# One exponential over four score tiles instead of two, and new slots for the order of the other work

## The reference

```python
q = (x @ Wq.T + bq).reshape(B, S, H, Dh)          # H = 16 heads, Dh = 8
v = (x @ Wv.T + bv).reshape(B, S, H, Dh)
buckets = sum over 6 hyperplanes of (qa . plane >= 0) * 2**n
scores = einsum('bhsd,bhtd->bhst', q, q) / sqrt(128)
attn = softmax(scores * (62 + same_bucket), axis=-1)
out = einsum('bhst,bhtd->bhsd', attn, v)
# per batch: x = x + layernorm(attention(layernorm(x)))
h = silu(tlin(x, w1, s1)) * tlin(x, w2, s2)       # 512 wide
h = gelu(tlin(h, h1, s)); h = gelu(tlin(h, h2, s))
# x = x + layernorm(tlin(h, w3, s3)), the input of the FFN being layernorm(x)
```

## Time and profile before

| | |
|---|---|
| three runs | 1417.3, 1417.64 (median), 1419.8 us |
| the profiled execution, its time | 1414.98 us |
| its span, first to last instruction | 1412.9 us |
| time outside the span | 2.1 us |
| mean granted TensorE clock | 0.972 |
| start of T0 of batch 0; last T63 | 28.16; 1321.3 us |
| a batch in the middle (batch 10, T0 to T0) | 81.24 us |

### The profile page before, as it was taken

How to read it: one execution, slowest core, us unless ns; L and a number is a source line. 1 busy time by engine, 2 the same in 40 slices (tenths; PEclk the granted TensorE clock), 3 DMA queues, 4 the chain that set the end, 5 groups by cost and what they waited for, 6 DMA issues and landing times. The chain is left out here.

```text
span 1412.9 us, 19983 instructions
## 1 busy us (share of the span) xinstructions
PE 1239.0 (88%) x5430; PEld 525.6 (37%) x5522; DVE 1228.3 (87%) x4013; ACT 1086.0 (77%) x1477; POOL 1241.7 (88%) x275
## 2 busy tenths in 40 slices
PE   4656899998989899998999999898999889898997
PEld 1211334343433434334343433434343333433343
DVE  5988999999999999999999999999999899989420
ACT  2353778879797987979788797979789797878852
POOL 2789999999999999999999999999998999999810
PEclk9877899999999999999999999999999999999999
DMA  4645444453545354354534544354444435442100
GB/s 112 186 119 150 106 123 125 118 149 94 150 118 149 95 138 135 111 135 123 143 99 126 149 112 134 113 154 111 124 127 117 141 102 143 118 131 86 53 8 8
DMA packets 89472, 167.20 MB, mean 118 GB/s; under 512 B 18192, under 2 KB 54288, under 8 KB 89360
## 3 DMA queue, kind: packets, MB, share of 16 engines
q1 hardware_dynamic: 89252, 165.62, 42.1%
q10 hardware_dynamic: 108, 0.30, 0.1%
HBM read 150.39 MB, written 15.47 MB: 117 GB/s over the span
## 5 line engine op out<-in xcount | busy, mean ns | idle before, releaser
L943 POOL TENSOR_TENSOR logits<-max_row,logits 128x4096 f32<-128x4096 f32 x128 | 1139.2, 8914 | 44.1 <-DMA max_row<-max_scratch 42.1
L776 DVE CUSTOM_DVE_ANT_0 logits<-s_bank,coeff 128x512 f32<-128x512 f32 x1024 | 691.6, 676 | 0.0
L999 ACT ACTIVATE logits<-logits 128x1024 f32<-128x1024 f32 x512 | 508.8, 1048 | 50.4 <-POOL logits L943 49.2
L726 DVE TENSOR_SCALAR coeff<-brow,bcol 128x516 bf16<-128x516 bf16 x1024 | 480.0, 469 | 68.2 <-PE s_bank L532 46.7
L532 PE MATMUL s_bank<-mov_stack,stat_stack 128*128 128x512 bf16 x932 | 329.9, 395 | 54.9 <-DVE rowmax L776 45.8
L552 PE MATMUL aux_bank<-logits,v_pad 128*32 128x512 f32 x2048 | 252.5, 611 | 37.9 <-ACT logits L999 30.2
L664 PE MATMUL f_bank<-hid_a,h_sb 128*128 128x512 f32 x512 | 246.4, 593 | 0.9 <-DVE hid_a L865 0.8
L674 PE MATMUL f_bank<-hid_b,h_sb 128*128 128x512 f32 x512 | 241.7, 598 | 3.6 <-ACT hid_b L1114 3.6
L532 PEld LDWEIGHTS s_bank<-mov_stack,stat_stack 128*128 128x128 bf16 x1024 | 99.5, 99 | 354.3 <-DVE rowmax L776 218.3
L1019 ACT COPY oT<-aux_bank 128x512 f32<-128x512 f32 x64 | 37.2, 582 | 157.4 <-PE aux_bank L552 150.3
L674 PEld LDWEIGHTS f_bank<-hid_b,h_sb 128*128 128x128 f32 x512 | 96.8, 192 | 89.3 <-issue 78.2
(11 more groups left out here) (105 smaller groups left out, 961.7 us busy)
## 6 DMA issues: line engine op xcount, KB each, us to landing
max_row<-max_scratch SPq DMA_DIRECT2D x128, 512.0 KB, 4.1
brow<-bucket_scratch SPq DMA_DIRECT2D x63, 522.0 KB, 6.4
mov_stack<-q_scratch SPq DMA_DIRECT2D x192, 96.0 KB
stat_stack<-q_scratch SPq DMA_DIRECT2D x189, 96.0 KB
max_scratch<-rowmax_T SPq DMA_DIRECT2D x512, 1.0 KB
q_scratch<-q_parts SPq DMA_DIRECT2D x16, 384.0 KB, 6.4
x_in<-in_x SPq DMA_DIRECT2D x16, 256.0 KB, 4.3
q_scratch<-q_parts SPq DMA_DIRECT2D x16, 256.0 KB, 7.0
```

What stands on the lines that cost most here:

```text
L726: nc.vector.tensor_scalar(coeff[:, k % 3, :].rearrange("p (r n) -> p r n", r=ROW_RUNS), brow[:, h // 4 % 2, h % 4, :, 0:RUN], bcol[:, b % ...
L776: nc.vector.tensor_tensor_reduce(out=logits[:, ring(b, k), :], in0=tile_bank(k)[:], in1=coeff[:, k % 3, 0:SEQ], scale=float(E) ** -0.5, sc ...
L943: nc.gpsimd.tensor_tensor(tiles, max_row[:, m % 2].unsqueeze(2).broadcast_to([P, GROUP, ST, SEQ]), tiles, ALU.subtract).then_inc(below_max ...
L999: nc.scalar.activation(logits[:, first:first + 2, :], logits[:, first:first + 2, :], ACT.Exp, scale=-1.0).then_inc(probs_done, 1)
```

## The change

One exponential covers the four tiles of a head: two instructions of 2048 columns to a group where there were four of 1024. PE's wait for them counts accordingly. Most slots have new values. The slots of work that the prediction speaks of:

```diff
-COPY_LAG = 35
+COPY_LAG = 36
-X_LOAD_SLOT = 14
+X_LOAD_SLOT = 29
-X_MOMENTS_SLOT = 42
+X_MOMENTS_SLOT = 38
-X_NORM_SLOT = 49
+X_NORM_SLOT = 48
-Q_SLOT = 60
+Q_SLOT = 59
-ATT_NORM_SLOT = 28
+ATT_NORM_SLOT = 27
-Y1_PREPARE_SLOT = 35
+Y1_PREPARE_SLOT = 36
 Y1_NORM_SLOT = 36
-END_STATS_SLOT = 44
+END_STATS_SLOT = 43
-END_PREPARE_SLOT = 50
+END_PREPARE_SLOT = 48
-END_NORM_SLOT = 58
+END_NORM_SLOT = 52
-EXP_SLOTS = (12, 13, 14, 15)
+EXP_SLOTS = (13, 15)
-GATE_SLOTS = (43, 44, 49, 50)
-UP_SLOTS = (47, 48, 51, 52)
+GATE_SLOTS = (44, 45, 49, 50)
+UP_SLOTS = (46, 47, 51, 52)
-FIRST_HIDDEN_SLOTS = (57, 57, 58, 60, 62, 62, 64, 64, 65, 67, 70, 73, 74, 74, 75, 75)
+FIRST_HIDDEN_SLOTS = (57, 57, 58, 60, 61, 61, 63, 64, 64, 67, 70, 72, 73, 73, 75, 75)
-SILU_SLOTS = (41, 47)
-MULTIPLY_SLOTS = (47, 47, 52, 52)
-OUTPUT_SLOTS = (102, 104, 105, 105)
+SILU_SLOTS = (44, 47)
+MULTIPLY_SLOTS = (46, 47, 52, 52)
+OUTPUT_SLOTS = (101, 102, 105, 105)
-STORE_SLOT = 4
-LOAD_SLOT = 5
-Q_STORE_SLOT = 24
+EXP_TILES = ST
+STORE_SLOT = 1
+LOAD_SLOT = 4
+Q_STORE_SLOT = 31
...
-                first = ring(b, m * GT) + 2 * n
-                nc.scalar.activation(logits[:, first:first + 2, :], logits[:, first:first + 2, :],
+                first = ring(b, m * GT) + EXP_TILES * n
+                nc.scalar.activation(logits[:, first:first + EXP_TILES, :], logits[:, first:first + EXP_TILES, :],
...
-                    for n in range(GT // 2):
+                    for n in range(GT // EXP_TILES):
```

More of the change, by code:

```diff
@@ L52 @@
 EPS = 1e-5
-GATE_SLOTS = (43, 44, 49, 50)
-UP_SLOTS = (47, 48, 51, 52)
-FIRST_HIDDEN_SLOTS = (57, 57, 58, 60, 62, 62, 64, 64, 65, 67, 70, 73, 74, 74, 75, 75)
-SECOND_HIDDEN_SLOTS = (81, 81, 82, 82, 82, 82, 86, 88, 88, 88, 91, 91, 92, 95, 95, 98)
-SILU_SLOTS = (41, 47)
-MULTIPLY_SLOTS = (47, 47, 52, 52)
-OUTPUT_SLOTS = (102, 104, 105, 105)
+GATE_SLOTS = (44, 45, 49, 50)
+UP_SLOTS = (46, 47, 51, 52)
+FIRST_HIDDEN_SLOTS = (57, 57, 58, 60, 61, 61, 63, 64, 64, 67, 70, 72, 73, 73, 75, 75)
+SECOND_HIDDEN_SLOTS = (81, 81, 82, 82, 82, 82, 86, 88, 90, 90, 90, 91, 93, 94, 96, 97)
+SILU_SLOTS = (44, 47)
+MULTIPLY_SLOTS = (46, 47, 52, 52)
+OUTPUT_SLOTS = (101, 102, 105, 105)
 FIRST_GELU_SLOTS = (65, 70)
@@ L73 @@
 PV_LAGS = (36, 36, 37, 37)
-COPY_LAG = 35
+COPY_LAG = 36
 TRANSPOSE_LAG = 39
 DIVIDE_LAGS = (38, 39)
-X_STATS_SLOT = 33
-X_MOMENTS_SLOT = 42
-X_PREPARE_SLOT = 41
-X_RSTD_SLOT = 47
-X_NORM_SLOT = 49
+X_STATS_SLOT = 32
+X_MOMENTS_SLOT = 38
+X_PREPARE_SLOT = 39
+X_RSTD_SLOT = 40
+X_NORM_SLOT = 48
 XNT_COPY_SLOT = 53
 XNT_SLOT = 58
-Q_COPY_SLOT = 57
-Q_SLOT = 60
-Q_HIGH_SLOT = 56
+Q_COPY_SLOT = 56
+Q_SLOT = 59
+Q_HIGH_SLOT = 55
 V_SLOT = 32
@@ L93 @@
 Q_REST_SLOT = 61
-PROJ_SLOT = 26
-BITS_SLOT = 26
+PROJ_SLOT = 27
+BITS_SLOT = 27
 Q_MIDDLE_SLOT = 59
@@ L98 @@
 BCOL_COPY_SLOT = 28
-Q_LOW_SLOT = 62
+Q_LOW_SLOT = 63
 ROW_SLOT = 42
@@ L103 @@
 ATT_STATS_SLOT = 24
-ATT_MOMENTS_SLOT = 25
-ATT_PREPARE_SLOT = 27
-ATT_RSTD_SLOT = 24
-ATT_NORM_SLOT = 28
-RESIDUAL_SLOT = 31
-Y1_STATS_SLOT = 32
-Y1_MOMENTS_SLOT = 33
-Y1_PREPARE_SLOT = 35
-Y1_RSTD_SLOT = 39
+ATT_MOMENTS_SLOT = 26
+ATT_PREPARE_SLOT = 26
+ATT_RSTD_SLOT = 28
+ATT_NORM_SLOT = 27
+RESIDUAL_SLOT = 30
+Y1_STATS_SLOT = 33
+Y1_MOMENTS_SLOT = 35
+Y1_PREPARE_SLOT = 36
+Y1_RSTD_SLOT = 37
 Y1_NORM_SLOT = 36
@@ L117 @@
 FFN_SLOT = 38
-END_STATS_SLOT = 44
+END_STATS_SLOT = 43
 END_MOMENTS_SLOT = 51
-END_PREPARE_SLOT = 50
+END_PREPARE_SLOT = 48
 END_RSTD_SLOT = 53
-END_NORM_SLOT = 58
-Y2_SLOT = 56
+END_NORM_SLOT = 52
+Y2_SLOT = 59
 SUB_SLOT = 8
-EXP_SLOTS = (12, 13, 14, 15)
+EXP_SLOTS = (13, 15)
 S_BANKS = 4
@@ L131 @@
 GT = GROUP * ST
-STORE_SLOT = 4
-LOAD_SLOT = 5
-Q_STORE_SLOT = 24
-FIRST_XNT_SLOT = 17
-FIRST_Q_STORE_SLOT = 36
-X_LOAD_SLOT = 14
-ROW_STORE_SLOT = 46
+EXP_TILES = ST
+STORE_SLOT = 1
+LOAD_SLOT = 4
+Q_STORE_SLOT = 31
+FIRST_XNT_SLOT = 16
+FIRST_Q_STORE_SLOT = 33
+X_LOAD_SLOT = 29
+ROW_STORE_SLOT = 45
 STACK_SLOT = 8
-FFN_LOAD_SLOT = 7
+FFN_LOAD_SLOT = 9
 FFN_LOAD_STEP = 3
 X_RES_SLOT = 49
-OUT_SLOT = 61
+OUT_SLOT = 63
 def sandwich_kernel(nc, x, wqT, bq, wvT, bv, hyper_blocks, hyper_bias, w1T, w2T, h1T, h2T, scales, w3T, w3_s, out):
@@ L548, in weigh_values @@
                         pe.wait_ge(att_done, b * QUADS + quad)
-                    pe.wait_ge(probs_done, b * (TILES // 2) + (quad + 1) * QT // 2)
+                    pe.wait_ge(probs_done, (b * TILES + (quad + 1) * QT) // EXP_TILES)
                 for hh in range(4):
```

## The result

The changed kernel takes 1449.91 us (median of 5 runs, 1448.26 to 1455.58) against 1417.3 us (5 runs, 1417.02 to 1419.8): a ratio of 1.0226 [1.0207, 1.0245], 32.6 us more. The forecast was 1428 with a range of 1407 to 1440. The sign of the forecast was right; the loss is three times the 11 us that it had. The profiled execution is the longest of the five, 1455.58 us, so shares and places are read from it, and sizes per batch from its usual batches.

The account below looks back on a forecast made before the run. No engine fills a batch; waits tie POOL (m0 to m2), ACT (to SQRT) and DVE (T54 to T8) into a loop. Twelve batches of 0.9 us plus small terms gave +11 us: 1428 us, range 1407 to 1440.

Parts of the forecast that it names:

- ACT from the second normalisation to SQRT: +0.6 us: On ACT, two long exponentials behind the normalisation replace three short ones, so SQRT comes 0.59 us late per batch.
- The exponentials: On ACT, a merged exponential of 2048 columns takes 1.91 us; a batch costs ACT 1.5 us less.
- T54 to T62: On DVE after SQRT, a late `xnT` copy and q matmul make it wait for S60 to S62: +0.5 us a batch.
- The load of x: On SP, moved behind m2's broadcast, so m0's broadcast lands sooner: -0.2 us a batch.
- T38: PE's transposes come late and DVE waits 0.7 us, hidden in what it waits at T44 and T54 now.
- The `end_rstd` wait: A sign in the changed profile: this wait above 1.2 us in most batches; its absence would speak against the forecast.
- A broadcast late by under 1 us is covered: At m5, behind the `x_res` load: costs nothing, as the scaling no longer holds POOL up before m6.
- (2): Both late terms, T54 to T62 and the stretch to SQRT, fall away: no change, 1417 us; chance 0.11.
- (3): Only the T54 to T62 term falls away: +6 us, 1423 us; chance 0.15.
- (4): The wait at T38 is longer than DVE's spare time and adds 0.7 us: 1438 us; chance 0.07.
- (1): Waits at T44 and T54 were the real loss, cleared by ACT's 1.5 us: 1397 us, or 1407 with half; chance 0.27.
- (5): A long exponential costs two short pitches, stretch to SQRT +1.0 us: 1433 us; chance 0.40 shared with the forecast.

Follow-up runs that it names:

- kernel 1: Changed kernel plus one tiny exponential of one column ahead of the second normalisation's wait for the bias, to load the table there: 1427.88 us, ratio 1.0062.
- kernel 5: Kernel before with only the exponentials merged over four tiles, at slots 12 and 14, other slots as before: 1429.83 us, ratio 1.0075.
- kernel 7: Changed kernel with the tiny exponential, the `x_res` load early, and the scaling of `ffn` back behind m4's exponentials (slot 58): 1420.4 us, ratio 1.0015.
- kernel 10: Kernel before with only SQRT moved ahead of the normalisation of x on ACT (slot 50 to 48): 1419.16 us, ratio 1.0002.
- kernel 2: Changed kernel with only the load of `x_res` back ahead of m5's maxima stores (slot 46 instead of 49): 1447.92 us, ratio 1.0209.
- kernels 2 and 3: Changed kernel with the `x_res` load early: alone 1447.92 us; in 3 together with the tiny exponential ahead of the bias wait, 1425.5 us.
- kernels 9 and 11: Against the kernel before: 9 merges only each group's last two exponentials and moves the load of x, 1414.41 us; 11 also puts SQRT first, 1412.66 us.
- kernel 8: Changed kernel with every long exponential cut back into two short ones side by side, all slots as changed: 1456.67 us, ratio 1.0272.
- 4, normalisation one slot sooner: Kernel before with only the second normalisation moved from slot 36 to 35, ahead of m2's first exponential: 1459.14 us, ratio 1.029.

## Why the prediction was wrong

The loop in four pieces, us, medians of batches 2 to 12 from the timelines. A tile starts here with DVE's multiplication of its bank (L776), and "bias" is the end of POOL's `att_bias` for the second normalisation.

| kernel | m0's subtraction to bias | bias to T54 | T54 to next T8 | T8 to m0's subtraction |
|---|---|---|---|---|
| before | 32.29 | 20.30 | 21.17 | 7.27 |
| changed | 32.31 | 22.30 | 21.67 | 7.24 |
| 1, load warmed up | 32.33 | 20.88 | 21.67 | 6.92 |
| 5, long ones alone | 32.88 | 20.38 | 21.09 | 7.91 |
| 7, scaling back | 32.29 | 20.88 | 21.06 | 7.10 |
| 10, SQRT first | 32.31 | 20.08 | 21.40 | 7.26 |

**The step that failed** is "ACT from the second normalisation to SQRT: +0.6 us", in the sentence "The rest is the same work in the same order". The work in front of the stretch was not looked at. I had counted the table changes of a batch, 13 and 13, and let them drop out of the sum; but the load of the exponential's table had run in ACT's waiting time, ahead of an exponential that ran "for nothing", and it went behind the normalisation with it. The cover that the prediction said was lost held 1.06 us of exponential and 1.28 us of load. The stretch grew by 2.0, not 0.59: 0.59 for the exponentials, 1.28 for the load, 0.1 left over. With the load taken out it grew by 0.58 (kernel 1), and the loss was 9.6 us where the forecast had 11. So the other terms of the sum held on the loop; that kernel 1's 1427.9 is the forecast's very 1428 is luck within an interval of some 3 us either way.

**Right.** The loop itself, read from the waits: what delays ACT between the bias and SQRT came out in every batch. The exponentials: 256 of 1906 ns mean, against 1.91 by the slope of the earlier trace rows. An estimate from the Trainium skill, "ScalarE: Activation LUTs", section "What ACT_TABLE_LOAD costs", is 186 + 2048 x 0.833 = 1892 ns, and the trace agrees within 1%. T54 to T62, forecast +0.5: from T54 to the next T8 it is +0.50 in the changed kernel and in kernel 1, and kernel 7 gives back 0.43 by its time. The load of x, forecast -0.2: m0's broadcast lands in 3.7 us instead of 3.9 to 4.0; no run moved this load alone. T38: hidden, as said; the waits there are 0.19 + 0.28 us where 0.7 was forecast. The wait of T44 for the bank is gone, and POOL's wait for the scaling is gone from the middle batches.

**Wrong beside it.** The `end_rstd` wait was to exceed 1.2 us; it stayed at 0.79, because DVE had been held up by as much at T43 to T46 already, by the `ffn` copy and the slow gates. In kernel 1, where these waits are gone, it is 0.79 too, and DVE waits 0.3 us each at T46 and T52 for its multiply. The prediction had looked at those places only for what they do to ACT, not for what a late ACT does to them. "A broadcast late by under 1 us is covered" (m5): it was late by 1.2 us or more (in the median POOL starts m5 8.4 us behind DVE's T48 in the changed kernel, 7.2 in kernel 2), and the rest of the 3.4 us is POOL coming early to a late DVE. It cost little; kernels 2 and 3 can't tell it from nothing. What makes five batches long in the changed kernel, some 10 us of its profiled execution, is not settled; kernel 1 has one such batch, with the `x_res` load in its place. POOL's wait for the m0 maxima did not vanish, as said, but fell from 0.7 to 0.4 us in the mean. The batch was to be near 82 us and is 83.1.

**Rivals.** None of the five was it, and the range did not hold the time. (2) and (3) fall with the term at T54 to T62, which came; (4) with the 0.5 us that DVE waited at T38. (1), a gain from a faster ACT, was nearest in kernels 9 and 11, but only after keeping the cover; its own condition, SQRT no later than 19.0 us after the bias, was met in kernel 10 (18.27) and brought nothing, so the wait at T54 was no loss of its own either. (5), a long instruction costing two short pitches, falls with the timeline, where two long ones take 3.71 us, a pitch of 1.80, and with kernel 8.

## What to carry to other kernels

Ahead of moving an instruction behind one that waits, list everything that ran in the waiting time with it, table loads too, though they belong to no line of the program. The load runs directly in front of the first activation that needs the table, and ahead of that activation's own wait, so a tiny activation of that table ahead of the wait puts it back under cover. A merged instruction is worth having where it delays no wait that another engine depends on, here the second half of each group (1414.4 us, with the load of x moved too) and not the first (1430).

## What the runs showed of the hardware

TensorE's granted clock fell more often at the gates where they came late, but idle time ahead of them doesn't decide it alone. The view of busy time by stretch, of PE alone, in batch 12 of the changed kernel (its columns: stretch and length, PE busy, granted clock, DMA share, GB/s):

```profile
1078.00:1081.50 3.50, 3.35 (x25) 1.00 0.21 78
1084.40:1086.00 1.60, 1.51 (x3) 0.68 0.42 123
1086.00:1088.00 2.00, 2.00 (x4) 0.50 0.02 4
1088.00:1089.50 1.50, 1.50 (x5) 0.87 0.00 0
1089.50:1091.00 1.50, 1.50 (x6) 1.00 0.00 0
```

After 2.90 us of idle time PE began the gates at 1084.49; its clock was 0.68 in the mean of the first stretch and 0.50, the 1.2 GHz level, in the next two microseconds, and back at 1.00 from 1089.5. The pair of gate products in between took 1.91 us; in kernel 1 it takes 1.02. Over batches 2 to 14 of each profiled execution, the clock was down to 0.50 during the first two pairs of gates as often as this:

| kernel | idle time of PE ahead of the gates, us | batches of 13 |
|---|---|---|
| before | 1.07 | 3 |
| 1, load warmed up | 1.48 | 0 |
| changed | 2.90, once 1.66 | 10 |
| 4, normalisation one slot sooner | 3.44 | 13 |
| 5, long ones alone | 0.25 to 0.46 | 8 |

In batches 6, 11 and 14 of the changed kernel 2.90 us of idle time left it at 1.00, and in kernel 5 it fell after less than 0.5 us. What else decides it is not shown. Where it fell, a late `ynT` copy was paid for twice, once as the wait and once in slow gates; DVE waited 0.65 us a batch for S46 behind them.
